# Local attention: queries and keys by token, normed and rotated there, then turned; weights times values on 64x64 tiles

## The reference, cut to what matters

```python
q = l2norm(q) * qs; k = l2norm(k) * ksc          # norm over the 64 channels of a head
q, k = rotary_xpos(q, k)                         # x * cos * scale + rotate_half(x) * sin * scale
# windows of 64 tokens; a window's queries see their own window and the one before
sim = einsum('bhwid,bhwjd->bhwij', bq * 8, bk)
sim = where((i < j) | (i > j + 64) | (j == -1), -max, sim)
out = einsum('bhwij,bhwjd->bhwid', softmax(sim), bv)
x = x + out.reshape(b, n, 512) @ wo
```

## Time and profile before

| | us |
|---|---|
| three runs | 2448.97, 2450.08, 2451.70 |
| median | 2450.08 |
| span of the profiled execution | 2427.7 |
| median less that span (start and end of an execution) | 22.4 |
| PE busy | 2292.7 (94%) |
| DVE busy | 1861.0 (77%) |
| ACT busy | 1802.1 (74%) |
| POOL busy | 1477.1 (61%) |
| four local-attention stages, first L368 to last L368 of each | 4 x 280.8 |

### The profile page before, as it was taken

One profiled execution on the slowest core, in us unless ns is written; L12 is line 12 of the kernel. 1 busy time (PEld: TensorE's weight loads), 2 busy tenths in 40 slices (PEclk: granted clock), 3 DMA queues, 4 the chain that ended last, 5 costly groups with the idle time before them and its releaser, 6 DMA issues. The chain is left out here.

```text
span 2427.7 us, 65264 instructions
## 1 busy us (share of the span) xinstructions
PE 2292.7 (94%) x21510; PEld 1689.7 (70%) x21510; DVE 1861.0 (77%) x4164; ACT 1802.1 (74%) x5994; POOL 1477.1 (61%) x1402
## 2 busy tenths in 40 slices
PE   5898999996898999999999999888999999999999
PEld 3894666663895888845888854774888864888863
DVE  4784888874786999955999964775999964999974
ACT  3455888883447999955999964337999973999982
POOL 5672777774674777733777740432787851878760
PEclk8897999998999999999999999999999999999999
DMA  6111000001112000000000000000000000000000
GB/s 243 45 45 38 2 0 0 0 1 41 45 45 98 7 6 9 4 5 3 8 8 6 6 1 1 1 1 7 8 6 9 6 1 5 11 6 6 9 1 35
DMA packets 34263, 47.49 MB, mean 20 GB/s; under 512 B 6384, under 2 KB 27760, under 8 KB 33744
## 3 DMA queue, kind: packets, MB, share of 16 engines
q1 hardware_dynamic: 29584, 36.45, 4.8%
q0 software_dynamic: 4544, 9.35, 1.2%
HBM read 24.44 MB, written 12.96 MB: 15 GB/s over the span
## 5 line engine op out<-in xcount | busy, mean ns | idle before, releaser
L265 POOL TENSOR_TENSOR space<-space,tabs 128x512 f32<-128x512 f32 x256 | 326.0, 1273 | 286.4 <-DVE space L369 270.0
L289 ACT ACTIVATE space<-psum,space 128x128 f32<-128x128 f32 x1024 | 357.6, 359 | 4.9 <-DVE space L373 4.9
L262 POOL TENSOR_TENSOR space<-space 128x512 f32<-128x512 f32 x256 | 266.2, 1040 | 149.2 <-DVE space L357 149.2
L269 POOL TENSOR_TENSOR space<-space 128x512 f32<-128x512 f32 x256 | 324.8, 1269 | 26.8 <-POOL space L265 7.6
L173 PE MATMUL psum<-space,big 128*128 128x256 f32 x1024 | 264.4, 381 | 10.4 <-DVE space L369 7.2
L1006 POOL TENSOR_TENSOR space<-space 128x256 f32<-128x256 f32 (+1 forms) x256 | 221.1, 884 | 85.5 <-DVE space L1107 83.4
L353 DVE CAST psum<-cb 128x512 f32<-128x512 bf16 x256 | 177.8, 694 | 87.8 <-ACT space L289 87.8
L1051 ACT ACTIVATE space<-psum,space 128x128 f32<-128x128 f32 (+1 forms) x512 | 209.7, 441 | 1.7 <-DVE space L1100 1.7
L196 PE MATMUL psum<-space,cf 128*128 128x384 f32 x512 | 208.6, 489 | 0.0
L289 ACT ACTIVATION_READ_ACCUMULATOR space<-psum,space 128x1 f32 x1024 | 205.3, 200 | 0.0
L173 PEld LDWEIGHTS psum<-space,big 128*128 128x128 f32 x1024 | 175.1, 191 | 29.9 <-issue 16.7
(11 more groups left out here) (193 smaller groups left out, 5636.1 us busy)
## 6 DMA issues: line engine op xcount, KB each, us to landing
big<-early SPq DMA_DIRECT2D x1, 6688.0 KB
space<-sorted_x SPq DMA_DIRECT2D x78, 64.5 KB, 1.9
z<-token_y SPq DMA_DIRECT2D x16, 256.0 KB, 5.6
space<-z SPq DMA_DIRECT2D x64, 64.0 KB, 1.9
space<-z SPq DMA_DIRECT2D x64, 63.8 KB, 2.0
big<-late SPq DMA_DIRECT2D x1, 3114.0 KB, 13.7
x<-x_t SPq DMA_DIRECT2D x4, 512.0 KB, 6.6
x_final<-x SPq DMA_DIRECT2D x8, 256.0 KB, 2.0
```

The costliest lines, as they stand in the source:

```text
L262: pool.tensor_tensor(x, x, rl[:, (j - 3) % 2, :, :].rearrange("p h t -> p (h t)").unsqueeze(2).to_broadcast([P, 4, P]), ALU.mult).then_inc ...
L265: pool.tensor_tensor(tS[:, :], t2[:, :], tab[:, 1, :], ALU.mult).then_inc(ts_ready, 1)
L269: pool.tensor_tensor(t3[:, j % 2, :], t1[:, j % 2, :], tS[:, :], ALU.add).then_inc(summed, 1)
L289: ins = act.activation(pr[:, (j - 3) % 2, h, t * P:(t + 1) * P], s_ps[h][:, t * P:(t + 1) * P], ACT.Exp, bias=nm[:, (j - 3) % 2, h, t:t + ...
```

## The change

- Queries and keys are made by token: `hT` of 128 tokens is the stationary operand, the weights of queries and keys (256 columns) the moving one, twice. Bank 0 then holds tokens on partitions, and for each half (t) of the tokens queries and keys of both heads.
- A head's channels now lie side by side, so the square sum is a DVE reduction of 512 squares to 8 numbers, Ln and Exp work on 8 columns, and `head64` with its two products is gone. The clamp is folded into the bias of Ln.
- Rotation: DVE multiplies bank 0 by the cosine table, and bank 0 with the halves of each head read in swapped order by the sine table; the shuffle is gone and GpSimd no longer multiplies by the sine table. GpSimd adds the two and, a step later, multiplies by the reciprocal root (8 numbers spread over 64 columns each).
- Four more transposes turn queries and keys; ACT copies them out as `qk` (one copy of 512 columns).
- The transposed weights now lie in one bank and are copied by ACT in one piece; DVE no longer takes part.
- Weights times values: eight products on 64x64 tiles. The upper 64 rows (first window of a tile) write bank 2, the lower 64 bank 6; ACT copies one half (`o0`), DVE adds the other to it. The mixed copy of the values (two ACT instructions) is gone.
- The running sums of the exponentials go to PSUM, and the reciprocal reads them there, ahead of the mask. The exponentials of a unit move one step earlier (s-2). The first score product has 64 columns instead of 128.
- The scores wait for `qk` and the mask themselves. The queues are reordered. `scaled_tabs` moves to GpSimd, ahead of the second routing.

The core of the diff:

```diff
@@ tensor_body
-                for n in range(2):
-                    ins = mm(qk_ps[:, n * T:(n + 1) * T], wq[:, n, j, :], hT[:, k, :], start=(n == 0), stop=(n == 1), skip_group_check=True)
+                for t in range(2):
+                    ins = mm(qk_ps[:, t * T:(t + 1) * T].rearrange("p (n c) -> p n c", n=2), hT[:, k, t * P:(t + 1) * P], wq[:, 0:2, j, :],
+                             start=(t == 0), stop=(t == 1), skip_group_check=True)
...
-                mm(ss_ps[:, 0:3 * P], g.head64[:, :], sq[:, (j - 1) % 2, 0:3 * P], start=True, stop=True, skip_group_check=True)
-                if runs(s - 2, U):
-                    pe.wait_ge(masked, S0 + s - 1)
-                mm(ss_ps[:, 3 * P:], g.head64[:, :], sq[:, (j - 1) % 2, 3 * P:], start=True, stop=True, skip_group_check=True).then_inc(ss_ready, 1)
...
+                pe.wait_ge(qk_ready, S0 + u + 1)
+                pe.wait_ge(masked, S0 + u + 1)
...
-                for q0, n, tile in ((0, P, 0), (P, WIN, 2), (P + WIN, WIN, 1)):
-                    for h in range(2):
-                        ins = mm(ol[h * LD:(h + 1) * LD, q0:q0 + n], v[:, j, tile, h * LD:(h + 1) * LD], pt[:, j % 2, h, q0:q0 + n],
-                                 start=(q0 == 0), stop=True, skip_group_check=True)
+                for spans in (((0, P, 0), (0, P + WIN, 0)), ((P, P, 1), (P + WIN, WIN, 1))):
+                    for r, (q0, n, tile) in enumerate(spans):
+                        rows = slice(r * WIN, (r + 1) * WIN)
+                        for h in range(2):
+                            ins = mm(ol[r][h * LD:(h + 1) * LD, q0:q0 + n], v[rows, j, tile, h * LD:(h + 1) * LD], pt[rows, j % 2, h, q0:q0 + n],
+                                     start=(q0 == 0), stop=True, skip_group_check=True)
...
+            if runs(s, U):
+                if at_least(s, 4):
+                    pe.wait_ge(o0_ready, S0 + s - 3)
+                for t in range(2):
+                    ins = mm(v_ps[:, t * P:(t + 1) * P], hT[:, k, t * P:(t + 1) * P], wq[:, 2, j, :], start=(t == 0), stop=(t == 1), skip_group_check=True)
...
+            u = s - 1
+            if runs(u, U):
+                pe.wait_ge(scaled, S0 + u + 1)
+                if at_least(u, 1):
+                    pe.wait_ge(qk_ready, S0 + u)
+                for n in range(2):
+                    for t in range(2):
+                        ins = nc.tensor.transpose(qkT_ps[:, n * T + t * P:n * T + (t + 1) * P], t3[:, (j - 1) % 2, t * T + n * P:t * T + (n + 1) * P], g.ident32)
+                ins.then_inc(turned, 1)
@@ gpsimd
+                    x = t3[:, (j - 1) % 2, :].rearrange("p (m d) -> p m d", m=8)
+                    pool.tensor_tensor(x, x, rn[:, (j - 1) % 2, :].unsqueeze(2).to_broadcast([P, 8, LD]), ALU.mult).then_inc(scaled, 1)
...
-                    pool.tensor_tensor(tS[:, :], t2[:, :], tab[:, 1, :], ALU.mult).then_inc(ts_ready, 1)
@@ scalar_body
+                act.activation(qk[:, j % 2, :], qkT_ps, ACT.Copy).then_inc(qk_ready, 1)
+                act.activation(pt[:, j % 2, :, :].rearrange("p h n -> p (h n)"), pt_ps, ACT.Copy).then_inc(pt_ready, 1)
+                act.activation(sq[:, j % 2, :], qk_ps, ACT.Square).then_inc(sq_ready, 1)
+                act.activation(lnn[:, (j - 1) % 2, :], ss[:, (j - 1) % 2, :], ACT.Ln, scale=float(2 ** 20), bias=g.tiny[:, 0:1]).then_inc(ln_ready, 1)
+                act.activation(rn[:, (j - 1) % 2, :], lnn[:, (j - 1) % 2, :], ACT.Exp, scale=-0.5, bias=g.tiny[:, 1:2]).then_inc(rn_ready, 1)
+                act.activation(o0[:, j % 2, :], ol[0], ACT.Copy).then_inc(o0_ready, 1)
...
+                act.activation(v[:, j, :, :].rearrange("p a b -> p (a b)"), v_ps, ACT.Copy).then_inc(v_ready, 1)
@@ vector_body
+                dve.reciprocal(rl[:, (j - 3) % 2, :, :], ls).then_inc(rl_ready, 1)
...
+                dve.tensor_copy(s_pair, band).then_inc(masked, 1)
...
+                dve.tensor_reduce(ss[:, (j - 1) % 2, :], sq[:, (j - 1) % 2, :].rearrange("p (m d) -> p m d", m=8), AX.X, ALU.add).then_inc(ss_ready, 1)
...
+                dve.tensor_tensor(t1[:, j % 2, :], qk_ps, tab[:, 0, :], ALU.mult)
+                dve.tensor_tensor(halves(t2[:, j % 2, :]), halves(qk_ps)[:, :, ::-1, :], halves(tab[:, 1, :]), ALU.mult).then_inc(rotated, 1)
...
+                dve.tensor_tensor(oT[:, j % 2, :], ol[1], o0[:, j % 2, :], ALU.add).then_inc(o_ready, 1)
```

More of the change, by code:

```diff
@@ L134, in steps, with begins @@
                 yield CH * (2 * i + k) + j, 2 * i + k, k, j
-    def elsewhere(s, only):
-        first = is_first(s) and head is not None
-        return first if only is None else s != only
+    def begins(s, only):
+        return runs(s, U) and (s == only if only is not None else not (is_first(s) and head is not None))
     def others(engine, eng, s):
@@ L160, in tensor_body @@
         for s, b, k, j in steps(i):
-            if elsewhere(s, only):
-                continue
-            if runs(s, U):
+            if not isinstance(s, int):
+                for n in (1, 3, 4):
+                    pe.compute_val(S0 + s - n)
+            if begins(s, only):
                 pe.wait_ge(h_there[k], H0 + 32 * (i + 1))
@@ L174, in tensor_body @@
                 ins.then_inc(proj_ready, 1)
[L176 to L195, removed]
-                mm(ss_ps[:, 0:3 * P], g.head64[:, :], sq[:, (j - 1) % 2, 0:3 * P], start=True, stop=True, skip_group_check=True)
-                if runs(s - 2, U):
-                    pe.wait_ge(masked, S0 + s - 1)
-                mm(ss_ps[:, 3 * P:], g.head64[:, :], sq[:, (j - 1) % 2, 3 * P:], start=True, stop=True, skip_group_check=True).then_inc(ss_ready, 1)
+            if only is not None:
+                continue
@@ L201, in tensor_body @@
             u = s - 2
             if runs(u, U):
[L203 to L206, removed]
+                pe.wait_ge(g.late_loaded, 16)
+                pe.wait_ge(qk_ready, S0 + u + 1)
+                pe.wait_ge(masked, S0 + u + 1)
+                for w, q0, spans in ((0, 0, ((0, 0, WIN),)), (1, LD, ((0, 0, P),)), (0, P, ((P, P, WIN), (P + WIN, WIN, WIN))), (1, P + LD, ((P, P, P),))):
@@ new lines, in vector_body @@
+            u = s - 2
+            if only is None and runs(u, U):
+                if is_first(u):
+                    prev.free(dve, 3)
+                    prev.free(dve, 4)
+                dve.tensor_copy(s_pair, band).then_inc(masked, 1)
+            u = s - 1
+            if only is None and runs(u, U):
+                dve.wait_ge(sq_ready, S0 + u + 1)
+                if at_least(u, 2):
+                    dve.wait_ge(ln_ready, S0 + u - 1)
+                dve.tensor_reduce(ss[:, (j - 1) % 2, :], sq[:, (j - 1) % 2, :].rearrange("p (m d) -> p m d", m=8), AX.X, ALU.add).then_inc(ss_ready, 1)
@@ new lines, in vector_body @@
+            u = s - 2
+            if only is None and runs(u, U):
+                dve.wait_ge(s_ready, S0 + u + 1)
+                dve.tensor_reduce(nm[:, j % 2, :, :], s_pair.rearrange("p h (t n) -> p h t n", t=2), AX.X, ALU.max, negate=True).then_inc(nm_ready, 1)
+            if begins(s, only):
+                if is_first(s):
+                    dve.wait_ge(g.tabled, 8)
+                dve.wait_ge(sq_ready, S0 + s + 1)
+                if at_least(s, 2):
+                    dve.wait_ge(summed, S0 + s - 1)
+                dve.tensor_tensor(t1[:, j % 2, :], qk_ps, tab[:, 0, :], ALU.mult)
+                halves = lambda x: x.rearrange("p (m a e) -> p m a e", m=8, a=2)
+                dve.tensor_tensor(halves(t2[:, j % 2, :]), halves(qk_ps)[:, :, ::-1, :], halves(tab[:, 1, :]), ALU.mult).then_inc(rotated, 1)
@@ L1590, in vector @@
         dve.wait_ge(table_ready, ONE + 1)
-        if turn == 1:
-            g.scaled_tabs(dve)
     def gpsimd(pool):
@@ L1596, in gpsimd @@
             spare_rows(pool)
+        else:
+            g.scaled_tabs(pool)
         pool.wait_ge(id_ready, ONE + 1)
@@ L1881, in program @@
         g.l1_wo = [g.l1_wo[:, l * CH * P:(l + 1) * CH * P].rearrange("p (c k) -> p c k", c=CH) for l in range(2)]
-        g.l1_tab = [tabs[:, l].rearrange("p a q n -> p a (q n)") for l in range(2)]
+        g.l1_tab = [tabs[:, l] for l in range(2)]
         g.l1_w1 = [g.l1_w1[:, l * 2 * HID:(l + 1) * 2 * HID] for l in range(2)]
```

220 lines of the change are left out of this document (98 added, 122 removed).

## The result

The changed kernel takes 2557.78 us (median of 4 runs, 2556.4 to 2564.02) beside 2449.52 for the kernel before on the same chip: a ratio of 1.0445, 95% interval 1.0425 to 1.0466. It is slower by 4.5%, where 2% faster was forecast, and lies outside the range of 2343 to 2456.

What follows compares the result with a forecast made beforehand. ACT full, PE nearly, tied by a ring of scores, maxima, exponentials and mask. Rings at 4.25 us instead of 4.456 over 252 steps save 52 us: 2450.1 - 52 = 2398 us, range 2343 to 2456.

Steps and rivals of the forecast that it cites:

- the walk through the waits: All waits of one step, followed from the scores' start: three rings within 0.1 us, the longest 4.24 to 4.29.
- The ordinary step: One step of the local-attention stages: 4.25 us instead of 4.456, 52 us less over 252 steps.
- Weights x values on four tiles: PE's product in each step: 16 passes with all four tiles running together, 0.60 us, at the other end 1.20.
- Rival 3: Weights x values: its row halves do not run together, 1.20 us instead of 0.60, total 2547; chance 11%.
- Scores: PE's score products in each step: 64 of 512 columns fewer, time taken as equal, 0.70 us.
- Ln and Exp of 8 columns: ACT in each step: 0.25 us each, in place of 1.35 for Ln and Exp of 512 columns.
- A: Ring between PE and ACT: scores, weights x values, `o0` copy, exponentials, values copy, `qk` copy, hand-over: 4.24 us.
- ring B: PE's own ring: scores, weights x values, `o0` copy, hand-over, values, two transpose groups, projection: 4.19 us, perhaps 4.29.
- C: Ring of scores, weights x values, `o0` copy, exponentials, then reciprocal, mask and hand-over to the next scores: 4.15 us.
- rival 4: PE's clock in the stages falls to 1.2 GHz through waits and added transposes: 3357, or 91 us more for a tenth; 3%.
- POOL, tables, fill and drain: POOL 3.35 to 3.58 us a step, less than the step; tables nothing, at most 10 us; fill and drain 0.
- The 22.4 us: Median of runs 2450.08 over the profiled span 2427.7; taken as a part the change does not touch.

Runs made afterwards that it cites:

- the early add: The changed kernel with VectorE's add to z moved up between the square sums and the maxima; 2346.37 us, ratio 0.9655 to the kernel before.
- the 1.0468: The changed kernel unchanged, measured again in another call; 2561.87 us, ratio 1.0468 to the kernel before.

## Why the prediction was wrong

The step that failed is the walk through the waits. "I walked through all waits of a step" was not so: I followed the steps that all 64 share, and passed over the wait of one in four, PE's `wo` for the add to `z`. My working put a quarter of `z` among DVE's busy time and gave it 0.08 us. As work that is right. As an instruction that another engine waits for, its place was what counted, and the change had moved it from the middle of DVE's step to its end. The condition on PE is a line that stands unchanged in the diff, and the block on DVE, unchanged too, had come to stand behind all others. By the rows of the prediction it could have been worked out: `wo` stands 1.3 after the scores; the add would end after the maxima, two rotation products and an add, 0.77 + 0.64 + 2 x 0.61 + 0.31 + 0.39 = 3.3, and the trace has 3.42 for the product's start. That is 2.0 late in 60 steps, 120 us, enough to turn 52 faster into about 70 slower. Measured, the pieces are 84 faster by the shorter steps (the early add's 0.9655), 115 slower by the late start and 84 slower by the clock: 115 slower together, the 1.0468.

Point by point:

- **The ordinary step**: forecast 4.25. It is 4.05 to 4.41 in the changed kernel, with medians of 4.09, 4.13 and 4.23 for the three steps between long ones in the first stage, and 4.15 in the mean with the add early; so 252 x 0.31 = 78 us, and 84 by the ratio of 0.9655, instead of 52. Without the one block, the kernel would have been inside the range and better than the point.
- **Weights x values on four tiles**: taken 0.60, is 0.60 (820.20 to 820.80). Rival 3, that the halves do not run together, is out. That its 2547 lies near the 2558 measured is chance.
- **Scores**: taken 0.70, are 0.43. The term was too large by 0.27: 0.07 of it are the 64 columns, and the rest, as argued above, is a hold that I read ahead of another tile shape and took for the product's own.
- **Ln and Exp of 8 columns**: taken 0.25 each, hold 0.34 and 0.20. Four exponentials: taken 1.51, hold 1.20, and the copy behind them takes 0.17 of that back.
- **Rings**: with the early add the mean step of 4.15 is within 0.1 of the lengths of A, B and C. That is in part luck, for the ring that set it, through ACT's copies and both groups of transposes, was not among them. That ring hangs on the same thing as ring B, PE's values waiting for the `o0` copy, and moving the values behind one group of transposes took 0.12 off.
- **The clock**: rival 4 had the event right (a lower level) and the cause wrong. It does not come from the transposes alone: 1.00 with eight of them in the stages of every run with the add moved or the wait filled. By this the rule of the Trainium skill named there (TensorE: Matmul & The Clock Gate, Part 4: PE-mode transpose) has no effect to be seen here. It follows PE's idle time in the long step, 49 times of 56; "PE waiting 0.2 to 0.3" was taken for all steps alike, where it is 2.3 in one of four.
- **POOL, tables, fill and drain**: as expected. GpSimd holds 1.04, 1.04 and 1.27 for its three instructions and waits more than before. The tables are done at 555.4, and the second routing's first scatter then still waits 19.37 for DVE.
- **The 22.4 us** between median and span were not the start and end of an execution. In the runs here the time stands 1.8 to 2.0 above the span of the same execution (2557.52 and 2555.7), so the profiled execution of the kernel before must have been a faster one; its time is not on record. The forecast does not suffer, since it kept the 22.4 on both sides.

The version with the early add and the values behind the transposes of the weights beats both kernels: 0.954 of the kernel before, 0.953 with the sums in SBUF.

## What to carry to other kernels

When a queue is reordered, list every instruction of it that another engine waits for, the rare ones too, and put down the time of each in the new order beside the time at which it is wanted. An instruction that is due once in four steps and costs 0.4 us may cost 3.3 us by its place. Where a step differs from its neighbours, a mean step hides it: look at the starts one by one, and at the groups behind a long wait for a lower clock.

## What the runs showed of the hardware

- After a wait in which PE was busy 1.11 of 3.42 us (2.31 idle at a stretch), the next 4.44 us had a granted clock of 0.62, and the groups took up to twice their time. So it went behind 49 of 56 such waits; behind seven the clock stayed at 1.00, and no run here shows why. Idle times of 0.69 and 0.86 in otherwise full steps left it at 1.00. Useless products in the 2.3 us kept it at 1.00 and made the kernel 84 us faster.
- Four Exp of 128 columns with running sums hold ACT 0.34 each with sums in SBUF and 0.30 with sums in PSUM, but the next instruction then holds 0.50 instead of 0.33: 1.70 both ways.
- ACT takes 0.30 to 0.31 for 8 columns where 256 take 0.36.
- The same 20 passes of score products hold PE 0.50 when products on tiles of the same shape follow, and 0.65 to 0.70 when another shape follows; that the shape is the cause is not shown by itself.
